# Converting and subtracting the activations of two slots in one VectorE instruction, in the first of five expert chunks

## What is computed

```python
# layer 2, recurrent part: xw = x @ Wx + b
next_h = jnp.tanh(xw_t + prev_h @ Wh)          # 128 steps, 16 sequences each

# layer 2, mixture of experts (E = 8, hidden width F = 512)
router_logits = einsum('bth,eh->bte', h, router_w)
topk_values, topk_indices = top_k(router_logits, 2)
topk_weights = softmax(topk_values)
h1 = gelu(einsum('bth,efh->btef', h, w1) + b1)
expert_outputs = einsum('btef,ehf->bteh', h1, w2) + b2
out = x + sum(take(expert_outputs, topk_indices) * topk_weights)
```

## Time and profile before

| what | us |
|---|---|
| median of 3 runs | 302.65 |
| lowest and highest | 301.67, 302.88 |
| span of the profiled execution | 301.2 |
| TensorE busy | 264.4 |
| VectorE busy | 258.8 |
| ScalarE busy | 215.6 |
| GpSimd busy | 76.2 |
| chunk 0 of the experts, from the span's start | 101.18 to 130.26 |

### The profile page before, as it was taken

The page is one execution under the profiler, slowest core; times in us unless marked ns, Lnnn a source line. Parts: engine busy times, 40 slices in busy tenths (PEclk is TensorE's granted clock), DMA queues, the critical chain, the costliest instruction groups (busy, mean ns, idle before and its releaser), DMA issues.

```text
span 301.2 us, 8834 instructions
## 1 busy us (share of the span) xinstructions
PE 264.4 (88%) x2716; PEld 205.5 (68%) x2716; DVE 258.8 (86%) x635; ACT 215.6 (72%) x455; POOL 76.2 (25%) x148
## 2 busy tenths in 40 slices
PE   4969940049989999999999999999999999999994
PEld 4824440016956777778888788888777887888874
DVE  4888999989898897779988799887799988889885
ACT  6367899998842677767777676667566766689892
POOL 3367997000025413011302112212110311101000
PEclk9989976557999999999999999999999999999999
DMA  6990443101500000000000000000001000001000
GB/s 186 314 310 4 84 94 76 28 0 35 90 17 2 0 3 1 0 2 2 19 0 0 2 3 26 2 0 0 1 2 30 8 0 0 2 1 37 0 2 27
DMA packets 24031, 10.63 MB, mean 35 GB/s; under 512 B 13355, under 2 KB 22982, under 8 KB 24006
## 3 DMA queue, kind: packets, MB, share of 16 engines
q1 hardware_dynamic: 23470, 10.05, 13.6%
q10 hardware_dynamic: 536, 0.26, 0.3%
HBM read 6.11 MB, written 1.05 MB: 24 GB/s over the span
## 4 chain that ended last, share of the span: by engine, by line
PE 79%; DVE 16%; issue 1%; ACT 1%; DMA 1%; SPq 0%; DVEq 0%
PE bank L893 78%; DVE peak L706 3%; DVE big L728 3%; DVE peak L633 2%; DVE big L711 1%; DVE big L744 1%; PE bank L937 1%; DMA y_sb<-in_cond 1%; PE bank L1017 0%; DVE big L746 0%; DVE wyT L779 0%; DVE pkm L626 0%; DVE big L738 0%; DVE x_sb L759 0%; DVE q L700 0%
## 5 line engine op out<-in xcount | busy, mean ns | idle before, releaser
L893 PE MATMUL bank<-big,wt 128*128 128x384 f16 (+2 forms) x480 | 124.8, 336 | 0.6 <-DVE big L872 0.5
L893 PE MATMUL bank<-wt,big 128*128 (+1 forms) x1536 | 111.5, 219 | 0.1
L872 DVE TENSOR_TENSOR big<-big 128x384 f16<-128x384 f32 (+2 forms) x160 | 93.2, 585 | 20.5 <-ACT big L594 16.1
L893 PEld LDWEIGHTS bank<-wt,big 128*128 128x128 f16 x1536 | 97.9, 97 | 16.2 <-issue 0.2
L592 ACT ACTIVATE big<-bank,miscT 128x384 f32<-128x384 f32 (+2 forms) x160 | 96.2, 602 | 15.3 <-PE bank L893 8.2
L893 PEld LDWEIGHTS bank<-q,wxh 128*128 128x128 f32 x254 | 44.4, 189 | 17.4 <-issue 3.4
L893 PEld LDWEIGHTS bank<-big,wt 128*128 (+1 forms) x480 | 50.0, 117 | 4.8 <-issue 1.1
L580 ACT ACTIVATE q<-bank (+1 forms) x112 | 20.6, 184 | 38.7 <-PE bank L893 37.9
L404 POOL CAST big<-q 128x64 f16<-128x64 f32 x32 | 13.2, 413 | 129.0 <-ACT q L580 126.5
L868 DVE CAST big<-big 128x512 f16<-128x512 f32 (+2 forms) x104 | 38.6, 372 | 4.8 <-ACT big L592 3.9
L827 DVE SCALAR_TENSOR_TENSOR wyT<-bank,gates,wyT 128x128 f32<-128x128 f32 x128 | 39.8, 343 | 1.0 <-issue 0.6
(11 more groups left out here) (165 smaller groups left out, 320.0 us busy)
## 6 DMA issues: line engine op xcount, KB each, us to landing
wnat<-in_w SPq DMA_DIRECT2D x8, 512.0 KB, 7.7
x_sb<-in_x SPq DMA_DIRECT2D x4, 256.0 KB, 4.3
out_block<-wyT SPq DMA_DIRECT2D x15, 64.0 KB
wn<-in_w_gate ACTq DMA_DIRECT2D x1, 192.0 KB, 4.9
wn<-in_w_up SPq DMA_DIRECT2D x1, 192.0 KB, 5.6
wn<-in_w_down SPq DMA_DIRECT2D x1, 192.0 KB, 5.7
b_in<-in_b SPq DMA_DIRECT2D x12, 4.0 KB
wt<-wyT SPq DMA_TRANSPOSE x8, 3.0
```

Of the source, the lines that this page charges most:

```text
L872: V.tensor_tensor(g_lo[:, par, f, 0:w], g32[:, f, 0:w], g_hi[:, par, f, 0:w], ALU.subtract).then_inc(g_lo_done, 1)
L893: return nc.tensor.matmul(o, l, r, start=start, stop=stop, skip_group_check=True)
```

## The change

A tuple `PAIRED = (0,)` names chunk 0. In that chunk VectorE does nothing for an even slot beyond its additions and router work, and at the odd slot it treats both: slots f = 0, 1 with one conversion and one subtraction of 128 x 2 x 256 elements, and slots f = 2, 3 with a conversion of f = 2 alone (ScalarE makes `g_hi` of f = 3 as before) and one subtraction of both. The conversion waits for the later slot's gelu, and `g_lo_done` rises by two at the end of the subtraction. The other chunks, and the programs of the other engines, are as they were.

```diff
+PAIRED = (0,)
 HI_SCALAR = ((3,), (3,), (3,), (3,), (0, 1, 3))
...
+            def split_two(c, e2, s, slot):
+
+                f, par, w = s % NF - 1, s // NF, WIDTHS[c]
+                by_vector = [g for g in (f, f + 1) if g not in HI_SCALAR[c]]
+                if by_vector:
+                    dve.wait_ge(g32_done, slot - f + by_vector[-1])
+                    at = slice(by_vector[0], by_vector[-1] + 1)
+                    V.tensor_copy(g_hi[:, par, at, 0:w], g32[:, at, 0:w]).then_inc(hi_v, len(by_vector))
+                    dve.wait_ge(hi_v, hi_made(c, e2, s, False))
+                if len(by_vector) < 2:
+                    dve.wait_ge(g_hi_done, hi_made(c, e2, s, True))
+                V.tensor_tensor(g_lo[:, par, f:f + 2, 0:w], g32[:, f:f + 2, 0:w], g_hi[:, par, f:f + 2, 0:w],
+                                ALU.subtract).then_inc(g_lo_done, 2)
...
                     if first and s == 6:
                         mix(c)
-                    if f not in HI_SCALAR[c]:
+                    if c in PAIRED:
+                        if f % 2 == 1:
+                            split_two(c, e2, s, slot)
+                    elif f not in HI_SCALAR[c]:
                         dve.wait_ge(g32_done, slot + 1)
                         V.tensor_copy(g_hi[:, par, f, 0:w], g32[:, f, 0:w]).then_inc(hi_v, 1)
                         dve.wait_ge(hi_v, hi_made(c, e2, s, False))
                     else:
                         dve.wait_ge(g_hi_done, hi_made(c, e2, s, True))
-                    V.tensor_tensor(g_lo[:, par, f, 0:w], g32[:, f, 0:w], g_hi[:, par, f, 0:w],
-                                    ALU.subtract).then_inc(g_lo_done, 1)
+                    if c not in PAIRED:
+                        V.tensor_tensor(g_lo[:, par, f, 0:w], g32[:, f, 0:w], g_hi[:, par, f, 0:w],
+                                        ALU.subtract).then_inc(g_lo_done, 1)
```

## The result

| | before | after |
|---|---|---|
| median of 20 runs, us | 302.47 | 303.58 |
| lowest and highest | 301.36, 303.22 | 302.43, 304.98 |
| profiled execution, span | 301.2 | 301.9 |

The ratio is 1.0035, with a 95% interval from 1.0023 to 1.0047. That is 1.06 us slower, between 0.70 and 1.42. The forecast was 0.57 us slower and "the same" within 0.5%; the direction, the range and the first place were right, the size was about half of what was measured.

What follows compares the result with a forecast made beforehand. TensorE was taken to set the pace in chunk 0, so VectorE savings booked no gain; the only term, 0.57 us of delay at slot 4, gave 302.65 + 0.57 = 303.2 us, range 302.2 to 304.1.

Steps and rivals of the forecast that it cites:

- The cover of 4.03 us: Chunk 0: the 2.7 us saved on VectorE lies beside TensorE's work, within 4.03 us of room, so no gain.
- VectorE time saved is worth nothing by itself: Chunk 0: only when each pair's first `g_lo` is ready counts; 0.68 us saved a turn books no gain.
- The joint conversion at 0.423 us: Chunk 0 on VectorE: converting 2 rows of 256 takes as long as 512 flat elements, 0.423 us.
- The first term, 0.57 us: Start of chunk 0: the joint subtraction ends later, so TensorE starts slot 4 at 104.31 instead of 103.74.
- 0.03 us for the signal: Start of chunk 0: time from the end of gelu of slot 1 to the joint conversion's start, 0.03 us.
- 0.04 to the next: Start of chunk 0: time from the joint conversion's end to the joint subtraction's start, 0.04 us.
- So nothing ahead takes up the delay: From slot 4 on: TensorE's matmuls follow without a gap, so the whole 0.57 us is kept.
- The rival of the swallowed delay: Loop turns: two or three TensorE holes of issue close and the 0.57 us is gone, 302.65 us; chance 16%.
- 0.18 us in hand: Third loop turn, slots 0 and 1: 0.33 us from subtraction to TensorE's request, less 0.15 for the signal.
- The rival that the change costs in each turn too: Loop turns: slow joint instructions use up the time in hand and TensorE waits there too, 303.7 us; chance 12%.
- that rival: Loop turns: VectorE was the bound after all, gaining up to 2.0 us against 0.57 lost, 301.2 us; chance 6%.
- the forecast's upper row: Clock case, chance 8%: 2.44 us without work preceded a clock of 0.57; after 0.88 us it stayed at 1.00.

Runs made afterwards that it cites:

- the flat block: The changed kernel with chunk 0's activations packed without gaps, each joint instruction one run of 512 elements; chunk length 30.76 us, ratio to before 1.0019.
- the kernel with the delay: The kernel before plus one unused VectorE subtraction of 1152 columns between conversion and subtraction of slot 0 of chunk 0; chunk length 32.37 us, ratio 1.0050.

## Why the prediction came out as it did

- **What bounds the kernel.** TensorE sets the pace in the loop turns: right. "Everywhere else in the chunk the subtraction is there before TensorE asks for it": wrong. At slot 3 of the first loop turn TensorE already lost 0.19 us to VectorE, and the table of waits lists it under "issue". The rows that would have shown it were in the trace: VectorE without a pause up to 109.46, and slot 1 to slot 3 at 1.73 us where later turns need 1.54.
- **The cover of 4.03 us** is misread. It is called the difference between the two busy times, but that is 28.04 - 25.05 = 2.99 us; 4.03 is the stretch of 29.08 less VectorE's busy time. Either is more than the 2.7 us saved, and an average over the chunk says nothing about the one turn in which VectorE had no pause.
- **VectorE time saved is worth nothing by itself:** held in the loop turns, not in the first. VectorE's busy time in the stretch of the chunk fell by 3.5 us (25.05 to 21.57, where some 2 were expected) and the kernel got slower. In the written-out turn the saved time let VectorE catch up from 0.72 us late to 0.03, and 0.19 us of the delay came back.
- **The joint conversion at 0.423 us, whatever its shape:** right, 0.427; the flat block is no different.
- **The first term, 0.57 us:** right in each step and in its place, measured 0.72. What failed are the small distances. The steps "0.03 us for the signal" and "0.04 to the next" were 0.11 and 0.10 in the kernel after, where both instructions count by two; that is 0.14 of the missing 0.15.
- **"So nothing ahead takes up the delay":** wrong by 0.19 us. The rival of the swallowed delay was right in this small part, with another mechanism: the hole of issue that closed was one that a late subtraction had made.
- **"0.18 us in hand" in the loop:** wrong. From the 0.33 us go 0.27 and not 0.15 from subtraction to down projection, and 0.13 more for the two late starts: 0.07 short. The rival that the change costs in each turn too was right, with another cause than slow instructions. Its size was 0.38 us over three turns, of which 0.08 stand at a place that is not explained, against the 0.2 over two that it was given with slow conversions.
- **The sum:** 0.72 - 0.19 + 0.38 = 0.91 us in the profiled chunk, inside the 0.70 to 1.42 of the runs. Whether the remaining 0.15 of the median is real can't be told. That the number fell inside the range is in part luck: the loop's 0.38 us were put at nothing and the first term was 0.15 short, and the 0.19 that came back hid some of it. The range, 1.9 us wide for the scatter of the runs, would have held a good many sums.
- **The rivals on either side.** VectorE was a bound in one turn of four, and its release through the pairs brought the 0.19 us above, not the 2.0 us of that rival. The clock did not fall after the 1.19 us of the changed kernel, but it did after 1.60, so the margin was far smaller than the 2.44 us of the forecast's upper row.

## What to carry to other kernels

Joining two instructions of a producer saves its fixed costs and delays the first of its two results; look at who needs that first result, and count the time in hand to the consumer at every turn, with the distance that this very pair of instructions shows in the same kind of turn. An engine that works without a pause can be the bound there even when no one reports a wait for it: compare the same slots in different turns. Where a consumer's wait is tied to more than it needs (here the bank wait), or another engine's work falls on the producer's busy stretch (here the bias split), moving these can be worth more than saving instructions: here the chunk got 0.67 us shorter by such moves and 0.91 longer by the joint instructions.

## What the runs showed of the hardware that was not expected

- VectorE's conversion that waits for gelu and raises a semaphore by two started 0.11 us after gelu's end, and 0.03 us after it when it raised it by one. The subtraction that raises by two started 0.10 us after its conversion, one that raises by one 0.04 us.
- From a subtraction's end to the start of the down projection that needs it, 0.06 us passed in the written-out turn, 0.14 at slot 2 and 0.26 to 0.28 at the slots of f = 0 in loop turns.
- A conversion of 384 columns took 0.98 us beside a GpSimd subtraction and 0.35 without it; a joint subtraction took 1.45 us beside one and 0.69 alone.
- The granted clock stayed at 1.00 after 1.19 us without matmuls. In the kernel with the delay, after 1.60 us without matmuls, it was 0.52 in the microsecond that begins 0.24 us after the restart, 0.50 in the next two, and 1.00 from 109 us on.
